# Graph attention and a top-2 expert layer on one core: expert work in one pass, and in two passes with each token's row scattered once

## What is computed

```python
def gnn(x, adj, mask, W, b, a1, a2, att_b):
    h = einsum('bni,di->bnd', x, W) + b
    logits = (h @ a1)[:, :, None] + (h @ a2)[:, None, :] + att_b
    att = sigmoid(logits) * adj * mask[:, :, None] * mask[:, None, :]
    att = att / (att.sum(-1, keepdims=True) + 1e-8)
    return einsum('bij,bjd->bid', att, h) * mask[:, :, None]

def ffn(x, gate_w, gate_b, w1, b1, w2, b2, gamma, beta):
    vals, idx = top_k(x @ gate_w + gate_b, 2)          # 2 of 16 experts
    weight = softmax(vals)
    h = relu(einsum('bsh,ehf->bsef', x, w1) + b1)      # 128 -> 256
    expert_out = einsum('bsef,efh->bseh', h, w2) + b2  # 256 -> 128
    y = x + sum_k weight_k * expert_out[idx_k]
    return layernorm(y) * gamma + beta

x = x + gnn(layernorm(x), adj, nodemask, ...)
x = x + ffn(layernorm(x), ...)
```

## Time and profile before

| | us |
|---|---|
| median of 3 runs (lowest, highest) | 455.33 (454.75, 459.12) |
| the profiled execution, its own time | 456.47 |
| span of its profile (first to last instruction) | 454.70 |
| PE busy | 343.6 (76%) |
| POOL busy | 303.0 (67%) |
| DVE busy | 295.3 (65%) |
| ACT busy | 228.1 (50%) |

### The profile page before, as it was taken

One profiled execution on the slowest core, in us unless ns is written; L12 is line 12 of the kernel. 1 busy time (PEld: TensorE's weight loads), 2 busy tenths in 40 slices (PEclk: granted clock), 3 DMA queues, 4 the chain that ended last, 5 costly groups with the idle time before them and its releaser, 6 DMA issues.

```text
span 454.7 us, 11203 instructions
## 1 busy us (share of the span) xinstructions
PE 343.6 (76%) x2287; PEld 279.0 (61%) x2287; DVE 295.3 (65%) x1466; ACT 228.1 (50%) x704; POOL 303.0 (67%) x331
## 2 busy tenths in 40 slices
PE   4688878877878854200998988988888889888992
PEld 3566767766767753100897777777777778833330
DVE  4687899999999884610476666666555555610664
ACT  3568869978999844100333333333333334311662
POOL 5620767777777777773277777777777777771565
PEclk9999989999999985555799999999999999999998
DMA  7812536645555643496866777777777776316994
GB/s 239 282 59 71 170 137 190 184 162 163 165 174 199 212 151 107 160 234 216 256 184 186 213 218 205 237 211 217 212 222 217 214 232 191 108 37 239 391 347 138
DMA packets 61683, 88.10 MB, mean 194 GB/s; under 512 B 10213, under 2 KB 40859, under 8 KB 61490
## 3 DMA queue, kind: packets, MB, share of 16 engines
q1 hardware_dynamic: 30786, 43.45, 32.5%
q0 software_dynamic: 10720, 25.32, 15.7%
q10 hardware_dynamic: 20112, 18.63, 13.8%
HBM read 55.61 MB, written 32.73 MB: 194 GB/s over the span
## 4 chain that ended last, share of the span: by engine, by line
PE 25%; DVE 20%; issue 13%; DMA 12%; POOL 12%; ACT 5%; ACTq 2%; DVEq 1%; POOLq 1%; SPq 0%
POOL token_y L445 8%; DMA token_y<-yb,xb 5%; PE psum L1265 5%; PE psum L1254 5%; DMA xb<-sorted_x 4%; POOL sorted_x L422 3%; ACT xn L535 3%; PE psum L1167 3%; PE psum L1298 2%; PE psum L1299 2%; DVE i L848 2%; PE psum L1157 2%; DMA out_dram<-xrow 1%; PE psum L1139 1%; DVE newton L812 1%
## 5 line engine op out<-in xcount | busy, mean ns | idle before, releaser
L445 POOL DMA_INDIRECT token_y<-yb,xb x143 | 143.3, 1002 | 58.1 <-issue 35.4
L422 POOL DMA_INDIRECT sorted_x<-xrow,rows x128 | 123.5, 964 | 60.1 <-issue 56.8
L606 ACT ACTIVATE hid<-psum,b_sb 128x256 f32<-128x256 f32 (+1 forms) x188 | 69.2, 419 | 142.7 <-PE psum L1254 72.0
L1265 PE MATMUL psum<-w_sb,hid 128*128 x572 | 83.1, 282 | 7.0 <-ACT hid L606 5.7
L1265 PEld LDWEIGHTS psum<-w_sb,hid 128*128 128x128 f32 x572 | 75.0, 192 | 15.5 <-issue 12.9
L1254 PE MATMUL psum<-xbT,w_sb 128*128 128x256 f32 (+1 forms) x376 | 81.7, 341 | 2.4 <-DVE xbT L1025 2.2
L1034 DVE TENSOR_TENSOR yb<-psum,b_bc 128x256 f32<-128x256 f32 (+1 forms) x94 | 33.9, 360 | 63.0 <-PE psum L1265 59.4
L1254 PEld LDWEIGHTS psum<-xbT,w_sb 128*128 128x128 f32 x376 | 58.2, 194 | 8.3 <-DVE xbT L1025 5.2
L1244 PE MATMUL psum<-ident_aug,xb 128*128 128x128 f32 x143 | 33.5, 292 | 29.6 <-DMA xb<-sorted_x 27.2
L1025 DVE COPY xbT<-psum 128x256 f32<-128x256 f32 (+1 forms) x94 | 33.2, 354 | 23.6 <-PE psum L1244 23.3
L1039 DVE SCALAR_TENSOR_TENSOR yb<-yb,xb 128x128 f32<-128x128 f32 x143 | 46.1, 351 | 3.3
(11 more groups left out here) (168 smaller groups left out, 567.6 us busy)
## 6 DMA issues: line engine op xcount, KB each, us to landing
xb<-sorted_x SPq DMA_DIRECT2D x49, 258.0 KB, 3.1
w_sb<-w_dram ACTq DMA_DIRECT2D x94, 128.0 KB, 2.9
adj_in<-adj_dram SPq DMA_DIRECT2D x32, 256.0 KB
got<-token_y SPq DMA_DIRECT2D x16, 512.0 KB, 5.7
xb<-sorted_x SPq DMA_DIRECT2D x45, 129.0 KB, 2.8
out_dram<-xrow ACTq DMA_DIRECT2D x16, 256.0 KB, 3.4
xmid<-x_dram SPq DMA_DIRECT2D x6, 512.0 KB, 8.0
token_y<-yb,xb POOLq DMA_INDIRECT x143
```

The costliest lines, as they stand in the source:

```text
L422: pool.indirect_dma_start(sorted_x, bass.IndirectOffsetOnAxis(ap=rows[:, slot, t, k:k + 1], axis=0), xrow[:, slot, k, t, :], None).then_in ...
L445: pool.indirect_dma_start(token_y, bass.IndirectOffsetOnAxis(ap=xb[:, q, t, TO:TO + 1].bitcast(I32), axis=0), yb[:, h, t, :], None, bounds ...
L606: last = act.activation(hid[:, u % RING, c, 0:n], psum[:, 2 + u % 2, c * BT:c * BT + n], ACT.Relu, bias=b1_sb[:, c, e])
L1265: last = mm(psum[:, 4 + u % 2, t * D:(t + 1) * D], hid[:, u % RING, c, t * P:(t + 1) * P], w2_sb[:, e, c * D:(c + 1) * D].rearrange("p a c ...
```

## The change

- **Two lists.** The expert work is done in two passes; list l holds every token's l-th choice, with its own ranks, counts, table and padding. Each pass has 17 blocks and 45 tails; one tail stands first alone, then the blocks, then 22 units of two tails (two experts, two row loads, two w1 loads): 40 units and 79 tiles a pass, 158 tiles in all.
- **A row goes out once and is sent on.** Stage 1 scatters each token once, as 134 floats (536 bytes: the normalised row, its place, both row numbers, both weights). In pass 1 DVE writes the result beside the row in its buffer, and POOL sends the whole 1,048-byte row to `sorted2` at the row of the second choice. Pass 2 adds its own result to it and sends 512 bytes to `token_y`, which now has one row for each token. Pass 2 loads nothing until all of pass 1 has landed.
- **Buffers.** A row buffer is now read, written and sent from; there are 8, and a buffer is loaded again only when the send of its unit has landed (`unit_out`). PE issues idle products (`hold_clock`) while it waits at the end of each pass.
- **Reciprocal roots** of the second layernorm and of the two late chunks move from DVE's 13 steps to POOL's four instructions (`rstd2_of`), into a doubled buffer.
- **ACT** normalises straight into the outgoing row; the copies are gone. The outgoing rows have 4 slots instead of 3.
- **Table entries** and padding rows are read up to eight at a time, without the instructions that assert their bounds.
- **Last stage:** 256 KB a group, and one product with the identity brings them into the accumulators (`copy_group`).

```diff
-IN_RING = 11
-OUT_RING = 8
+UNITS = ((FULL,),) + tuple((b,) for b in range(FULL)) + tuple(
+    (FULL + i, FULL + i + 1) for i in range(1, TAILS, 2))
+IN_RING = 8
+BATCH = 8
...
-XROWS = 3
-SCATTERS = TPP * TOPK
+XROWS = 4
+TO, ROW1, ROW2, WEIGHT1, WEIGHT2 = range(D, D + 5)
+RW = D + 6
+RW2 = D + RW
+SCATTERS = TPP
...
+            def load_unit(l, u, rows):
+                q = u % IN_RING
+                if l or u >= IN_RING:
+                    sp.wait_ge(unit_out[q], 16 * (sent(u - IN_RING, l) if u >= IN_RING else sent(last_in(q), 0)))
...
+                n = tiles_of(u) // loads_of(u)
+                for t, row in enumerate(rows.of(u)):
+                    if l == 0:
+                        sp.dma_start(xb[:, q, t:t + n, D:RW2],
+                                     sorted1[bass.ds(row, n * P), :].rearrange("(p t) c -> p t c", t=n)).then_inc(unit_in[q], 16)
+                    else:
+                        sp.dma_start(xb[:, q, t:t + n, :],
+                                     sorted2[bass.ds(row, n * P), :].rearrange("(p t) c -> p t c", t=n)).then_inc(unit_in[q], 16)
...
+            def rstd2_of(i):
+                s = i % 2
+                pool.wait_ge(var2_done, i + 1)
+                if i >= 2:
+                    pool.wait_ge(xn2_done, i - 1)
+                step(g.tensor_scalar(var2[:, s, 0, :], mv2[:, s, :, 1], EPS, None, ALU.add))
+                n = step(g.tensor_scalar(var2[:, s, 1, :], mv2[:, s, :, 0], -1.0, None, ALU.mult))
+                pool.wait_ge(pool_step, n)
+                n = step(g.tensor_tensor(rs2[:, s, 0, :], var2[:, s, 0, :], neg_half[:, 0:TPP], ALU.pow))
+                pool.wait_ge(pool_step, n)
+                g.tensor_tensor(rs2[:, s, 1, :], var2[:, s, 1, :], rs2[:, s, 0, :], ALU.mult).then_inc(rstd2_done, 1)
...
+            for m in range(4, PAIRS + 2):
+                if m <= PAIRS:
+                    rstd2_of(m - 1)
+                scatter(m - 2)
+                if m in (6, 7):
+                    rstd1_of(m + 1)
...
+                    if l == 0:
+                        pool.indirect_dma_start(
+                            sorted2, bass.IndirectOffsetOnAxis(ap=xb[:, q, t, D + ROW2:D + ROW2 + 1].bitcast(I32), axis=0),
+                            xb[:, q, t, :], None, bounds_check=PAD_ROW - 1, oob_is_err=False).then_inc(unit_out[q], 16)
+                    else:
+                        pool.indirect_dma_start(
+                            token_y, bass.IndirectOffsetOnAxis(ap=xb[:, q, t, D + TO:D + TO + 1].bitcast(I32), axis=0),
+                            xb[:, q, t, 0:D], None, bounds_check=TOKENS - 1, oob_is_err=False).then_inc(unit_out[q], 16)
...
             def turn(m):
                 residual(m - 1, graphs(m, 0) if valid(m) else ())
-                r = variance(m - 1, graphs(m, 1) if valid(m) else ())
-                norm_route_and_place(r, m - 2)
+                variance(m - 1, graphs(m, 1) if valid(m) else ())
+                route(m - 2)
+                place_pair(m - 2)
...
-                mm(y_v, ident[:, :], got[:, q, :, 0, :], start=True, stop=False)
-                mm(y_v, ident[:, :], got[:, q, :, 1, :], start=False, stop=True).then_inc(summed, 1)
+                mm(psum[:, bank, :].rearrange("p (t c) -> p t c", c=D), ident[:, :], got[:, q, :, :], start=True, stop=True
+                   ).then_inc(summed, 1)
```

More of the change, by code:

```diff
@@ L436, in _ @@
-            for i in range(PAIRS):
-                turn(i, i % XROWS)
-            def send(u):
-                q, h = u % IN_RING, u % OUT_RING
-                pool.wait_ge(yb_done, u + 1)
+            rstd2_of(0)
+            rstd1_of(5)
+            rstd2_of(1)
+            scatter(0)
+            rstd2_of(2)
+            scatter(1)
+            rstd1_of(6)
+            for m in range(4, PAIRS + 2):
[4 more added lines that the diff above has]
+                    rstd1_of(m + 1)
@@ L453, in finish @@
+            for l in range(LISTS):
+                for u in range(len(UNITS)):
+                    send(l, u)
             def finish(i):
@@ L499, in weigh @@
                 act.wait_ge(chosen_done, i + 1)
-                for k in range(TOPK):
-                    last = act.activation(xrow[:, slot, k, :, WEIGHT], lead[:, :], ACT.Sigmoid, scale=1.0 - 2.0 * k)
+                act.copy(xrow[:, slot, :, TO].bitcast(I32), result_row[:, i * TPP:(i + 1) * TPP])
+                for k, column in enumerate((WEIGHT1, WEIGHT2)):
+                    last = act.activation(xrow[:, slot, :, column], lead[:, :], ACT.Sigmoid, scale=1.0 - 2.0 * k)
                 last.then_inc(xrow_done, 1)
@@ L553, in turn @@
                 if valid(m - 2):
-                    keep(m - 2)
                     weigh(m - 2)
@@ L579, in _ @@
             transposed(3)
-            keep(0)
             keep_h(3, 0, 1)
@@ L1051, in _ @@
             dve.wait_ge(b2_in, 16)
[L1052 to L1060 removed]
+            for l in range(LISTS):
+                experts = Entries(mybir.EngineType.DVE, l, 1)
+                experts.of(0)
+                experts.of(1)
+                for u in range(len(UNITS) + 2):
+                    if u in (2, 3):
+                        unit_y(l, u - 2, experts.of(u - 2))
+                    if u < len(UNITS):
+                        unit_x(l, u)
+                    if u >= 4:
+                        unit_y(l, u - 2, experts.of(u - 2))
+                    if l == 0 and u % 2 == 0 and 0 <= u // 2 - 3 < GROUPS:
+                        add_beta(u // 2 - 3)
             def scale(g):
@@ L1259, in layer2, with layer1 @@
-            def layer2(u, e):
-                pe.wait_ge(hid_done, u + 1)
-                if u >= 2:
-                    pe.wait_ge(yb_done, u - 1)
+            def layer1(l, u):
+                w, q, n = l * len(UNITS) + u, u % IN_RING, tiles_of(u) // loads_of(u) * P
+                pe.wait_ge(xbT_done, w + 1)
+                pe.wait_ge(w1_in[q], 16 * loaded(u, l))
+                if w >= 2:
+                    pe.wait_ge(hid_done, w - 1)
+                for t in range(loads_of(u)):
+                    for c in range(FC):
+                        last = mm(psum[:, 2 + w % 2, c * BT + t * P:c * BT + t * P + n],
+                                  w1_sb[:, q, t, c * P:(c + 1) * P], xbT[:, w % RING, t * P:t * P + n],
+                                  start=True, stop=True)
+                last.then_inc(l1_done, 1)
```

675 lines of the change are left out of this document (315 added, 360 removed).

## The result

The change made the kernel slower: 476.18 us median of 4 runs (474.94 to 476.29) against 455.79 of the kernel before on the same chip, a ratio of 1.042 with a 95% interval of 1.0385 to 1.0455. The forecast was 448 with a range of 431 to 464. The profiled execution took 474.94 us, its span 472.4. The span grew by 17.7 us where the sum said 7.1 less, so 24.8 us have to be found.

The account below looks back on a forecast made before the run. DVE was taken to bound stage 1, POOL's scatter backlog the stretch after, POOL's issue the passes; -13.9 - 17.4 + 30.1 - 5.9 = -7.1 on 456.47 gave 449.4, less 1.14 for the median, 448 us, range 431 to 464.

Parts of the forecast that it names:

- the loop of stage 1: Stage 1: POOL's scatters and root, PE's transposes and DVE's row numbers close a loop of 16.44 us over two turns.
- Rival C: Stage 1: POOL's root instructions run longer beside DVE's, loop 1.16 us longer, 8.80 a turn, 455.5 us in all; chance 0.18.
- Rival B: Stage 1: POOL is no part of the loop, PE sets the turn at 7.4 us, 437.5 in all; chance 0.20.
- three turns at 0.52: Stage 1: each turn falls from 8.74 to 8.22 us, 0.52 less; thirteen such turns give 6.8.
- 4.6 - 1.0 for the two late chunks: Stage 1: DVE's two late chunks go, 4.6 us less; POOL's instructions in their place give 1.0 back.
- hidden behind the scatters: Last turn to first load: the table, ready at 23.8 us, lies behind the scatters by about one us.
- a read of eight costs 0.27 to 8 x 0.27 = 2.2 us, behind eight units of lead: Passes: batched table reads have eight units of lead; removing SP's 0.27 us reads was counted as nothing.
- the 3.10 of the earlier trace: Last turn to first load: the last pair's scatters land 3.10 us after their four issues, at 25.0 us.
- covered by the loads already in the ring: 0, at most 3 us: Passes: the second list's 16 padding transfers on SP's queue behind unit 12 cost 0, at most 3 us.
- a gain of 1.2 us of clock: Between the passes: idle products hold PE's clock, taking 1.2 us off 6.6 (bounds 0 and 3.3).
- Rival D: Passes: the ring of eight row buffers bounds them instead of POOL; at a 23.5 us round 25 more, 473; chance 0.16.
- the bound of the ring: Last stage: the ring of four stores bounds an interval at 6.0 / 4 = 1.5 us; 1.55 taken.

Follow-up runs that it names:

- e5: Scatters one turn later, with five outgoing-row slots instead of four, against the changed kernel: 469.05 us, ratio 1.025.
- e9: First list's padding issued only when all scatters have landed, against the changed kernel: 483.51 us in one run.
- e8: Second list's 16 padding transfers moved behind the first pass's last row load, against the changed kernel: 469.47 us, ratio 1.0266.
- e4: Ten slots of rows and of w1 instead of eight, against the changed kernel: 467.75 us, ratio 1.0248.
- e1: Idle products at the end of a pass cut from 4, 4 and 2 to 2, 2 and 1, against the changed kernel: 471.96 us, ratio 1.0305.
- f3: Last stage's stores issued by SP instead of ACT, against the version with short hold, single reads, later scatters and ten slots: 454.64 us, ratio 0.9954.
- e3: Table entries read one at a time instead of eight, against the changed kernel: 475.28 us, ratio 1.0386.
- e2: Second list's padding issued one transfer behind each of units 8 to 23 instead of two blocks, against the changed kernel: 477.65 us, ratio 1.0427.
- g2: One idle product behind each group's product in the last stage, against the best combination of edits: 452.84 us, ratio 0.9926.

## Why the prediction was wrong, point by point

**Right: the loop of stage 1.** It was put at 16.44 us for two turns, 8.22 a turn; 8.17 was measured over the six turns from 105.48 to 154.47, and e5 shows that it was this loop. POOL's root takes 1.95 us from 104.86 to 106.81 beside a working DVE, as in the earlier trace rows, and the instruction that raises to a power 1.037 to 1.085 us in all sixteen turns. Rival C had each of the root's four instructions wait out 0.29 us. The wait is there, but it is rare and short: where one of the short instructions starts just behind a DVE instruction with two inputs from SBUF it is longer, as here, with 0.33 us for the usual 0.23, beside DVE's L905 from 121.77 on:

```profile
121.81 0.33 POOL L503 TENSOR_SCALAR var<-mv 128x4 f32<-128x4 f32 x1
```

None of the 64 instructions of the sixteen roots is more than 0.14 us longer than usual, so rival C falls by its size. The rule of the Trainium skill that stood behind it (SBUF — State Buffer, Who interferes with whom) is that the two contend; the trace agrees with that much, by 0.14 us at most. Rival B came true only in e5, where the loop was cut: 7.48 a turn against its 7.4.

The 2.8 us that the stretch missed lie around this loop, and the row numbers on DVE (L749 before, L839 after) show where. The first pair's come at 42.76 instead of 44.44, 1.7 us sooner where 3.5 were forecast. From the fifth pair's to the eighth's 31.6 us became 29.4 (84.45 to 116.07 before, 78.17 to 107.59 after), 2.2 less where the sum had 5.2: three turns at 0.52, and 4.6 - 1.0 for the two late chunks. The step that failed is this 1.0: the chunks now stand on POOL's queue inside the loop (1.67 us at 84.90 and at 95.16, both in the chain), and there they cost the turns about what they had cost on DVE. The other turns gave 2.0 more than forecast, so the small miss of the whole stretch is in part luck. No run took this apart.

**The size off: from the last turn to the first load, 2.9 us.** The table was given 7.9 us and took 9.4. The step "hidden behind the scatters" and "a read of eight costs 0.27 to 8 x 0.27 = 2.2 us, behind eight units of lead" failed at the first use: before the first load no lead exists, and the chain reads

```profile
183.56 0.69 DVE tab L1036
184.27 1.68 SPq L309
185.98 0.53 SPq L309
...
186.92 2.32 DMA xb<-sorted
```

2.7 us from the table to the load, where the sum had the 0.87 that lay between the scatter's landing and the load. The last row numbers came 16.7 us into the stretch against 15.9. These are 0.8 + 1.5 + 1.8 = 4.1 us; the miss is smaller by luck, because the sum put the scatters' end 1.27 us too late: the 3.10 of the earlier trace rows counts from the start of the last scatter, three intervals behind the first one and not four, and without that the table would have been last and the forecast 1.1 us shorter. The scatter's landing, taken as these 3.10, ends about then too (its longest in the changed kernel is 6.7 us): the row was taken long after the padding was done, and beside the padding the landing takes more than twice as long (e9). That is why shortening the reads alone gained nothing there.

**Wrong: the passes, 13.6 us.** The sends were right (1.02 and 0.99 us and 0.30 to the next, against 1.31; the second pass took 105.1 against 104.2). Three steps around them failed. The start took 10.2 us from load to first send against 8.6: in the chain PE works on the second unit before it ends the first, and that unit now has two tiles where it had one, so its transposes, copy and products take 0.64, 0.44 and 2.08 us instead of 0.23, 0.30 and 1.22, which makes 1.4 of the 1.6. The second list's padding was costed as "covered by the loads already in the ring: 0, at most 3 us"; the first pass took 112.2 against 104.9, and e8 gives 5.3 of these 7.3 back, e4 5.0, overlapping. The idle products were reckoned only as a gain of 1.2 us of clock, never as work that the next rows wait behind: the turn-around took 13.5 us against 9.7, and e1 gives 3.3 back.

Rival D named the first pass's mechanism, a round of eight slots that grows until it passes 21 us, with landings of 3.6 and 3.1 us as its worst; 4.5 to 5.3 were seen. Its price of 25 us for both passes was too high: landings of 4.4 and 4.3 us stand in the chain of the second pass too (340.29 and 344.88), and yet that pass took only 0.9 us more than forecast. Most of the miss was elsewhere.

**Wrong: the last stage, 5.5 us.** The first scale came 9.9 us after the load's start where 7.3 were forecast, again behind the idle products: e1 wins 3.4 there. Its groups in DVE's timeline:

```profile
440.15 1.13 DVE L1093 SCALAR_TENSOR_TENSOR z<-psum,rs,gamma_bc 128x128 f32<-128x128 f32 x4
...
449.94 1.13 DVE L1093 SCALAR_TENSOR_TENSOR z<-psum,rs,gamma_bc 128x128 f32<-128x128 f32 x4 [2.24 <-DMA out_dram<-z]
...
464.91 1.13 DVE L1093 SCALAR_TENSOR_TENSOR z<-psum,rs,gamma_bc 128x128 f32<-128x128 f32 x4
```

24.8 us for 15 intervals, 1.65 each against 1.55: at times a store's landing holds them up (2.24 us here), as the bound of the ring had it, but with a landing of 5.9 us (443.90 in the chain) where it took 3.4 for all; their median is 2.2. ACT, for which no bound was worked out, stands in the chain at other groups: its squares begin 1.71 us apart (457.67, 459.38), with the root and the issue of a store between, and f3, which took the stores from it, won 1.1 us of the groups' span at most. From the last scale to the end 7.5 us went by against 6.1.

**What stays open.** Of the 24.8 us runs took back 6.6 (the idle products) and 5.3 (the padding); the rest is read from rows and was not tested by a run of its own. e3 alone could not be told from no effect in time. The end is 1.4 us longer behind the start of the last store (467.4 after, 451.1 before): 5.0 us to the end of the span against 3.6. Why, and what the ring of stores costs, was not tried.

## What to carry to other kernels

A change that takes work off a saturated queue also takes away the wait behind which other things were hidden: before, 16 us of backlog covered the padding and the table, and after it the table's reads and a landing that the padding makes long stood on the path. When a stage is made shorter, price again what it had covered, with durations taken beside the traffic that will be there then. A filler that is to hold the clock is work like any other: count when it ends against when the next operand can arrive.

## What the runs showed that was not expected

- A read of eight table entries took 1.71 us median on SP and 1.94 on PE's sequencer, a read of one 0.275. Batching saves some of the time per entry (all 124 entries took SP 23.2 us in 18 reads, and 37.3 in the 124 of e3), but the first load waits for a whole read (1.68 us in the chain at 184.27). The Trainium skill, Runtime: NRT & Kernel Launch, Instruction fetch mechanics, puts a load of registers at about 200 ns for each even in bulk, for loads from HBM; the table lies in SBUF here, and the trace agrees, 1.71 / 8 = 0.21 us.
- A scatter's landing goes from 2.5 us or less to 6.7 to 9.0 us when padding transfers start beside it.
- In the profiled executions of e2, e3 and e8 one turn of stage 1 (from about 66 us on) took 11.9 us where that of the changed kernel took 8.7. PE had been busy about half of the 4 us before in all of them, and its granted clock was 0.50 between 66 and 70 us in those three, 1.00 in the other. A difference of 3 us in stage 1 between single profiles of this kernel is therefore no evidence about an edit.
- One idle product a group kept TensorE's granted clock at 1.00 in the last stage and gained nothing: PE was then busy throughout and set the pace itself, 1.72 us a group (g2).
